# Identity products in TensorE's waits during the opening stage of an audio tower

## The chip, the cores and the metric

The kernel runs on one NeuronCore of a Trainium2 chip. The metric is device time in microseconds (us) of one execution, and lower is better. Five engines work side by side: TensorE (PE in the profile; its weight loads are listed apart as PEld), VectorE (DVE), ScalarE (ACT), GpSimd (POOL) and SyncE (SP), which issues most of the transfers. They meet at semaphores alone.

## The reference

Three blocks run one after the other on `x` of shape (8, 64, 1000):

```python
xp = x.reshape(B, C, S, 200)                       # 5 patches of 200 samples per channel
fr = jnp.fft.rfft(xp, axis=-1)
feats = jnp.concatenate([jnp.abs(fr), jnp.angle(fr)], axis=-1)
h = gelu(feats @ W1 + b1) @ W2 + b2                # tokens, 320 per batch row
...
dt = jnp.mean(jnp.clip(jnp.exp(log_dt), 0.0001, 1.0))
inv_term = jnp.linalg.inv(I - 0.5 * dt * A)        # 32 x 32
A_bar = (I + 0.5 * dt * A) @ inv_term
state = jnp.tanh(state @ A_bar.T + ub_t)           # 320 steps
...
h_new = z * h + (1.0 - z) * c                      # gated recurrence, 320 steps
```

The second and third block each add their result to `h`. The change touches the first block and the start of the inverse.

## The kernel before, in words

Every engine has a program written out by hand, and each runs its own list strictly in that order; what comes first anywhere is set by that order and by the semaphores.

The patches come in four pieces of `x` (`g` = 0 to 3). For a piece, VectorE (GpSimd for pieces 2 and 3) folds each patch into an even and an odd half (`even_odd`, L472 to L474), TensorE turns these into columns (`transposes`, L1217; two halves `h` of the piece, 6 and 4 products), ScalarE and VectorE copy them from PSUM (`evenT` L658, `oddT` L902), and TensorE multiplies them with a cosine and a sine table (`spectra`, L1231). Magnitude and angle are then worked out on three engines: VectorE reads the spectra (`imag` L908, `neghalf` L910), ScalarE takes absolute values, squares and roots, VectorE forms a reciprocal (`rdenom` L926), GpSimd multiplies (`absim` L568), ScalarE takes the arctangent, GpSimd and VectorE put the angle together (`angT` L937). ScalarE loads a new function table for each of root, arctangent and gelu (L688 with `ACT_TABLE_LOAD`).

The inverse is found by a Newton iteration with 40 steps of two halves each: `newton(i)` is one small product on TensorE (L1245 for even `i`, L1247 for odd `i`), and ScalarE copies its result back (L694, L697, L698) before the next half can start. The first eight halves (`EARLY`) stand in the opening stage, the others are spread between the products of the first network.

These are `up` (L1372: features times `W1`, magnitude half and angle half, 128 hidden units by up to 384 tokens) and `down` (L1387: times `W2`), in groups `n` = 0 to 6 of tokens and seven pieces `m` of hidden units. With the first `up` the opening stage ends. From about 180 us on, the gated recurrence with its 320 steps fills the rest of the span.

TensorE's list begins with `WARM` = 26 transposes of the identity matrix into PSUM bank 6, which nobody reads (L1251); they need the identity alone, which GpSimd has made by 1.6 us. Behind them stand the transposes of piece 0, which need the first load. The products are float32; a product that is no transpose stands in the profile as two matmuls.

Of the kernel before, what the change touches and what calls it, by code (L numbers as in the profile page):

```python
# [33 lines left out]
TINY_POWER = 1e-34  # L34
EPS = 1e-5
NEWTON = 40
WARM = 26
EARLY = 8

XT_PIECE, SKIP_PIECE = 4, 6  # L40
# [29 lines left out]
def audio_tower(nc, x, W1, b1, W2, b2, A, Bm, C, D, log_dt, W_out, b_out,  # L70
# [31 lines left out]
    with ExitStack() as ctx:  # L102
        def sb(name, shape, dt=F32):
            return ctx.enter_context(nc.sbuf_tensor(name, shape, dt))

        def sem(name):
            return ctx.enter_context(nc.semaphore(name))
# [7 lines left out]
        ident = sb("ident", [128, 128])  # L115
# [105 lines left out]
        def bank(i, p=128, w=512):  # L221
            return ps[0:p, i, 0:w]
# [3 lines left out]
        def ps_patT(k, g, h):  # L226
            return bank(k + (4 if (g, h) == (0, 1) else 0), KP - 1 if k else KP + 1)

        def ps_re(g, h):
            return bank(6 if (g, h) == (0, 1) else 2, NF, HT)  # L230

        def ps_im(g, h):
            return bank(7 if (g, h) == (0, 1) else 3, NF, HT)
# [42 lines left out]
        im_read = sem("im_read")  # L276
# [84 lines left out]
        def patches(h):  # L361
            s0, s1 = (0, S0) if h == 0 else (S0, NS)
            return s0, s1, slice(128 * s0, 128 * s1)
# [78 lines left out]
        def newton_bank(i):  # L442
            at = [key[0] for key, j in SLOTS.items() if j == i]
            b = 3 if i < EARLY else 2 if at[0] % 2 else 7
            return bank(b, 128, N), bank(b, 128, 2 * N)
# [760 lines left out]
        def _(pe):  # L1206
            mm, tr = nc.tensor.matmul, nc.tensor.transpose
            def transposes(g, h):
                s0, s1, cols = patches(h)
                if h == 0:  # L1210
                    pe.wait_ge(parts_done[g], 1)
                if 2 * g + h > 1:
                    pe.wait_ge(patT0_copied, 2 * g + h)
                    pe.wait_ge(patT1_copied, 2 * g + h)
                for k, part in enumerate((even, odd)):
                    for sg in range(s0, s1):
                        last = tr(ps_patT(k, g, h)[:, (sg - s0) * 128:(sg - s0 + 1) * 128],  # L1217
                                  part[:, g, sg, :], ident[:])
                last.then_inc(patT_psum, 1)

            def spectra(g, h):
                if h == 0:
                    if g == 0:
                        pe.wait_ge(dft_in, 48)
                    pe.wait_ge(patT0_copied, 2 * g + 2)
                    pe.wait_ge(patT1_copied, 2 * g + 2)
                if 2 * g + h > 1:
                    pe.wait_ge(re_read, 2 * g + h)
                    pe.wait_ge(im_read, 2 * g + h)
                for dst, table, part in ((ps_re(g, h), cos_sb, evenT), (ps_im(g, h), sin_sb, oddT)):  # L1230
                    last = mm(dst, table[:], part[:, h * HT:(h + 1) * HT], start=True, stop=True)  # L1231
                last.then_inc(spec_psum, 1)

            def wait_newton(i):
                if i % 2:
                    pe.wait_ge(xy_done, i + 1)
                else:
                    pe.wait_ge(dn_done, i // 2 + 1)

            def newton(i):  # L1240
                ps_nt, ps_nx = newton_bank(i)
                if i:
                    wait_newton(i - 1)
                if i % 2 == 0:
                    mm(ps_nt, step_w[:], Xn[:], start=True, stop=True).then_inc(nt_psum, 1)  # L1245
                else:
                    mm(ps_nx, DY[:], DY[:, 0:2 * N], start=True, stop=True).then_inc(nx_psum, 1)  # L1247

            pe.wait_ge(consts, 1)
            for _ in range(WARM):  # L1250
                tr(bank(6)[:, 0:128], ident[:], ident[:])  # L1251
            transposes(0, 0)
            transposes(0, 1)
            pe.wait_ge(su_dve, 2)
            pe.wait_ge(consts, 16)
            mm(bank(3)[:, 0:1], ones_row[:], dtsum[:], start=True, stop=True).then_inc(su_pe, 1)
# [2 lines left out]
            pe.wait_ge(su_dve, 9)  # L1259
            mm(bank(5)[0:N, 0:1], ones_sq[:], sqsum[:], start=True, stop=True).then_inc(sq_psum, 1)  # L1260
            spectra(0, 1)
            pe.wait_ge(su_dve, 11)
            pe.wait_ge(bf_ident, 4)
            pe.wait_ge(im_read, 1)
# [2 lines left out]
            pe.wait_ge(re_read, 1)  # L1267
            mm(bank(2)[:, 0:3 * DM], ones_row[:], vec_rows[:].rearrange("p a d -> p (a d)"),
               start=True, stop=True).then_inc(su_pe, 1)
            newton(1)  # L1270
            tr(bank(5)[:, 0:128], Wout_sb[:], ident[:]).then_inc(su_pe, 1)
            newton(2)
            transposes(1, 0)
            for i in range(3, 6):
                newton(i)
            pe.wait_ge(rows_in, 16 * 8)
            tr(bank(4)[:, 0:32], bias_rows[:], ident[0:32, 0:32]).then_inc(bias_psum, 1)
            for i in range(6, EARLY):
                newton(i)
            pe.wait_ge(su_act, 6)  # L1280

            def ssm_input(c):
# [352 lines left out]
```

## Time and profile before

| what | value |
|---|---|
| median of 3 runs | 895.92 us (894.9 to 898.41) |
| the profiled execution's own time | 894.79 us |
| its span, first to last instruction | 893.0 us |
| TensorE busy | 829.9 us, 93% of the span |
| mean granted TensorE clock | 0.581 of full speed |

The span leaves out 1.79 us around the instructions. The granted clock is 1 at 2.4 GHz and 0.5 at 1.2 GHz, the two levels that occur; a value between them is a mean over a stretch in which the level changed.

### The profile page before, as it was taken

The page shows a single profiled execution, that of the slowest core. Times are in us where ns is not written, and L with a number is a line of the kernel's source. Part 1 is how long each engine was busy: PE and PEld are TensorE (multiplying, and loading weights), DVE is VectorE, ACT ScalarE, POOL GpSimd, SP SyncE. Part 2 cuts the span into 40 slices and gives each one's busy share as a digit, 9 for nine tenths or more (in the row PEclk, how much of TensorE's full clock was granted, in tenths as well). Part 3 has the DMA queues.
Part 4 walks back from the last instruction along what each step waited for, and adds up shares of the span by engine and source line. Part 5 has one row for each costly group of instructions (what it writes and reads, how often), then busy time and mean ns, then how long its engine had stood idle before and what let it go on. Part 6 is the DMA issues. An engine that isn't in the chain of part 4 may idle for free.

```text
span 893.0 us, 40450 instructions
## 1 busy us (share of the span) xinstructions
PE 829.9 (93%) x17013; PEld 700.3 (78%) x17013; DVE 578.6 (65%) x3480; ACT 369.8 (41%) x2016; POOL 89.7 (10%) x205
## 2 busy tenths in 40 slices
PE   7889999989999999999999999999999998988875
PEld 5667666778888888888888888888888887877765
DVE  5243527376676776767767777677667777676654
ACT  5465766433343433433434334334333343343222
POOL 4212204110000000100000001000000000000000
PEclk6699999955555555555555555555555555555555
DMA  7100000000000000000000000000000000000000
GB/s 173 35 1 1 1 1 1 1 3 3 7 3 7 6 4 6 7 3 7 4 6 7 3 7 6 4 6 3 7 6 4 6 7 3 6 4 5 6 3 8
DMA packets 7452, 8.51 MB, mean 10 GB/s; under 512 B 1343, under 2 KB 6557, under 8 KB 7271
## 3 DMA queue, kind: packets, MB, share of 16 engines
q1 hardware_dynamic: 6965, 5.92, 2.8%
q8 instruction: 133, 2.18, 1.0%
q14 instruction: 48, 0.39, 0.1%
q0 software_dynamic: 256, 0.01, 0.0%
q10 hardware_dynamic: 50, 0.00, 0.0%
HBM read 4.62 MB, written 1.31 MB: 7 GB/s over the span
## 4 chain that ended last, share of the span: by engine, by line
PE 85%; ACT 6%; DVE 4%; issue 3%; DMA 1%; POOL 0%; POOLq 0%
PE ps L1511 42%; PE ps L1517 11%; PE ps L1313 8%; PE ps L1372 5%; PE ps L1423 3%; PE ps L1387 3%; PE ps L1525 3%; DVE h_hi L478 2%; PE ps L1431 2%; ACT addend L866 2%; PE ps L1295 1%; PE ps L1302 1%; PE ps L1283 1%; PE ps L1231 1%; PE ps L1247 1%
## 5 line engine op out<-in xcount | busy, mean ns | idle before, releaser
L1511 PE MATMUL ps<-h_hi,w_first 128*128 128x8 f16 x2552 | 267.3, 170 | 28.4 <-DVE h_hi L478 28.0
L1511 PEld LDWEIGHTS ps<-h_hi,w_first 128*128 128x128 f16 x2552 | 219.9, 104 | 90.9 <-DVE h_hi L478 90.9
L1511 PE MATMUL ps<-h_hi,w_rest 128*128 128x8 f16 x5104 | 276.3, 168 | 0.0
L1511 PEld LDWEIGHTS ps<-h_hi,w_rest 128*128 128x128 bf16 x5104 | 240.6, 105 | 0.1
L856 ACT ACTIVATE tanh_r<-ps 128x16 f32<-128x16 f32 x320 | 58.6, 183 | 252.3 <-PE ps L1517 251.7
L1517 PE MATMUL ps<-h_lo,w_first 128*128 128x8 f16 x2560 | 160.0, 168 | 0.1
L1511 PE MATMUL ps<-rh_hi,w_first 128*128 128x8 f16 x1276 | 136.6, 173 | 12.1 <-DVE rh_hi L1133 1.0
L1511 PEld LDWEIGHTS ps<-rh_hi,w_first 128*128 128x128 f16 x1276 | 109.6, 104 | 39.0 <-DVE rh_hi L1133 1.3
L1511 PE MATMUL ps<-rh_hi,w_rest 128*128 128x8 f16 x2552 | 138.6, 168 | 0.0
L478 DVE TENSOR_TENSOR_SCAN h_hi<-coef,addend 128x32 f16<-128x32 f32 x320 | 73.1, 228 | 85.7 <-ACT addend L866 85.7
L1511 PEld LDWEIGHTS ps<-rh_hi,w_rest 128*128 128x128 bf16 x2552 | 121.8, 105 | 0.0
L1517 PEld LDWEIGHTS ps<-h_lo,w_first 128*128 128x128 f16 x2560 | 117.9, 105 | 0.4 <-DVE h_lo L1156 0.2
L1133 DVE SCALAR_TENSOR_TENSOR rh_hi<-tanh_r,hseq 128x16 f16<-128x16 f32 x320 | 56.1, 175 | 90.0 <-ACT tanh_r L856 85.2
L866 ACT ACTIVATE addend<-ps 128x16 f32<-128x16 f32 x320 | 59.5, 186 | 110.1 <-PE ps L1517 100.7
L858 ACT ACTIVATE tanh_z<-ps 128x16 f32<-128x16 f32 x320 | 58.6, 183 | 77.7 <-PE ps L1517 77.7
L1313 PE MATMUL ps<-x2T,WuT 128*128 128x128 f32 x240 | 90.0, 480 | 0.3 <-ACT ps L780 0.3
L1517 PE MATMUL ps<-rh_lo,w_first 128*128 128x8 f16 x1280 | 79.3, 168 | 0.7 <-DVE rh_lo L1138 0.7
L602 POOL COPY hchunk<-hseq 128x128 f32<-128x128 f32 x40 | 11.7, 293 | 522.1 <-DVE h_lo L1156 522.1
L478 DVE TENSOR_TENSOR_SCAN hseq<-coef,addend 128x32 f32<-128x32 f32 x320 | 63.8, 199 | 0.0
L1156 DVE TENSOR_TENSOR h_lo<-hseq,h_hi 128x16 f16<-128x16 f32 x320 | 56.0, 175 | 11.0
L1138 DVE TENSOR_TENSOR rh_lo<-rh,rh_hi 128x16 f16<-128x16 f32 x320 | 55.9, 175 | 10.9
L739 ACT ACTIVATE states<-ps 128x8 f32<-128x8 f32 x320 | 55.2, 173 | 17.2 <-PE ps L1295 16.6
(211 smaller groups left out, 1421.6 us busy)
## 6 DMA issues: line engine op xcount, KB each, us to landing
x_sb<-in_x SPq DMA_DIRECT2D x4, 500.0 KB
out<-res SPq DMA_DIRECT2D x20, 64.0 KB, 2.0
W_sb<-in_L_tok_W SPq DMA_DIRECT2D x1, 606.0 KB
W_sb<-in_L_tok_W SPq DMA_DIRECT2D x1, 384.0 KB
wnat<-in_L_ffn_Wwr SPq DMA_DIRECT2D x1, 256.0 KB, 5.4
wnat<-in_L_ffn_Wwz SPq DMA_DIRECT2D x1, 256.0 KB, 11.2
wnat<-in_L_ffn_Ww SPq DMA_DIRECT2D x1, 256.0 KB, 10.5
wunat<-in_L_ffn_Wur SPq DMA_DIRECT2D x1, 128.0 KB, 6.9
```

The costliest lines, as they stand in the source:

```text
L478: return v.tensor_tensor_scan(out=dst, data0=coef[:].rearrange("p s i -> p (s i)"), data1=addend[:].rearrange("p s i -> p (s i)"), initial ...
L739: a.activation(states[:, c % 2, k * NB:(k + 1) * NB], ps_s[:, c % 2, k, :], ACT.Tanh, scale=1.0 / S_SCALE).then_inc(s_done, 1)
L856: a.activation(halves(tanh_r[:]), gate(c, j, 0), ACT.Tanh, scale=0.5 / G_SCALE).then_inc(r_done, 1)
L858: a.activation(halves(tanh_z[:]), gate(c, j, 1), ACT.Tanh, scale=0.5 / G_SCALE).then_inc(z_done, 1)
L866: a.activation(halves(addend[:, :, 0]), gate(c, j, 2), ACT.Tanh, scale=1.0 / G_SCALE).then_inc(c_done, 1)
L1133: v.scalar_tensor_tensor(out=rh_hi[:], in0=tanh_r[:], scalar=1.0, in1=h_prev, op0=ALU.add, op1=ALU.mult).then_inc(rh_hi_done, 1)
L1138: v.tensor_tensor(rh_lo[:], rh[:], rh_hi[:], ALU.subtract).then_inc(rh_lo_done, 1)
L1156: v.tensor_tensor(h_lo[:], hseq[:, j, :, 1], h_hi[:, :, 1], ALU.subtract).then_inc(h_lo_done, 1)
L1313: mm(gate_columns(g, c)[:, m].rearrange("p t b -> p (t b)"), WuT[:, i, :], x2T[:], start=False, stop=True, skip_group_check=True)
L1372: last = mm(ps_hid[p % 2][0:k, 0:nq * CT], W1_sb[:, half, m * 128:m * 128 + k], feats[:, t0:t0 + nq * CT], start=half == 0, stop=half == 1)
L1511: mm(gate(c, j, g, m), w[:, m * 128:(m + 1) * 128], state[:, k * NB:(k + 1) * NB], start=False, stop=False, skip_group_check=True)
L1517: last = mm(gate(c, j, g, m), w_first[:, g, k, m * 128:(m + 1) * 128], state[:, k * NB:(k + 1) * NB], start=False, stop=k == KH - 1, skip_ ...
```

## The change

`WARM` grows from 26 to 52, and groups of 6 or 12 more identity transposes (`BUSY` = 6) are put at ten places of TensorE's opening list: 78 products, 104 more with those of `WARM`. They write PSUM banks that are free at that place and signal nothing. Ahead of the first group into bank 7, TensorE now waits until VectorE has read that bank (`im_read`, 2). No other engine's list changes.

```diff
-WARM = 26
+WARM = 52
+BUSY = 6
...
+            def busy(count, b):
+                for _ in range(count):
+                    tr(bank(b)[:, 0:128], ident[:], ident[:])
+
             pe.wait_ge(consts, 1)
-            for _ in range(WARM):
-                tr(bank(6)[:, 0:128], ident[:], ident[:])
+            busy(WARM, 6)
             transposes(0, 0)
             transposes(0, 1)
+            busy(BUSY, 6)
             pe.wait_ge(su_dve, 2)
...
             spectra(0, 1)
+            busy(2 * BUSY, 0)
             pe.wait_ge(su_dve, 11)
...
                start=True, stop=True).then_inc(su_pe, 1)
+            busy(BUSY, 0)
             newton(1)
             tr(bank(5)[:, 0:128], Wout_sb[:], ident[:]).then_inc(su_pe, 1)
+            busy(BUSY, 0)
             newton(2)
             transposes(1, 0)
             for i in range(3, 6):
+                busy(BUSY, 4)
                 newton(i)
...
             for i in range(6, EARLY):
+                if i == 6:
+                    pe.wait_ge(im_read, 2)
+                busy(2 * BUSY, 7)
                 newton(i)
+            busy(BUSY, 7)
             pe.wait_ge(su_act, 6)
```

TensorE's list at its beginning, before (L1251 the identity products, L1217 the transposes of piece 0, L1256 the sum for `dt`, L1231 the spectra, L1260 a norm, L1245 the first Newton half):

```order
L1251 MATMUL ps<-ident 128x128 x26
L1217 MATMUL ps<-ident,even 101x128 x3
L1217 MATMUL ps<-ident,odd 99x128 x3
L1217 MATMUL ps<-ident,even 101x128 x2
L1217 MATMUL ps<-ident,odd 99x128 x2
L1256 MATMUL ps<-dtsum,ones_row 128x1
```

The same place in the change, where line numbers are one to thirteen higher (L1252 is the identity product, L1218 the transposes):

```order
L1252 MATMUL ps<-ident 128x128 x52
L1218 MATMUL ps<-ident,even 101x128 x3
L1218 MATMUL ps<-ident,odd 99x128 x3
L1218 MATMUL ps<-ident,even 101x128 x2
L1218 MATMUL ps<-ident,odd 99x128 x2
L1252 MATMUL ps<-ident 128x128 x6
L1261 MATMUL ps<-dtsum,ones_row 128x1
```

There are now 52 products ahead of the first transposes and 6 between them and the sum for `dt`.

TensorE's list at the end of the opening stage, before, from Newton half 5 on (L1277 turns the bias rows; the last row is the first `up` product):

```order
L1247 MATMUL ps<-DY 128x64
L1277 MATMUL ps<-ident,bias_rows 128x32
L1245 MATMUL ps<-Xn,step_w 128x32
L1247 MATMUL ps<-DY 128x64
L1372 MATMUL ps<-magT,W_sb 128x384
```

The same place in the change:

```order
L1248 MATMUL ps<-DY 128x64
L1286 MATMUL ps<-ident,bias_rows 128x32
L1252 MATMUL ps<-ident 128x128 x12
L1246 MATMUL ps<-Xn,step_w 128x32
L1252 MATMUL ps<-ident 128x128 x12
L1248 MATMUL ps<-DY 128x64
L1252 MATMUL ps<-ident 128x128 x6
L1385 MATMUL ps<-magT,W_sb 128x384
```

Twelve identity products stand ahead of Newton half 6, twelve between halves 6 and 7, and six ahead of the first `up` product.

## Rows read from the trace of the kernel before

**Rows 1.** The page: TensorE's busy time, and its granted clock in 40 slices (tenths).

```profile
PE 829.9 (93%) x17013; PEld 700.3 (78%) x17013; DVE 578.6 (65%) x3480; ACT 369.8 (41%) x2016; POOL 89.7 (10%) x205
...
PEclk6699999955555555555555555555555555555555
```

**Rows 2.** Busy time by stretch: us, PE, PEld, DVE, ACT, POOL (count), clock, DMA.

```profile
8.00:10.00 2.00, 1.30 (x6) 1.31 (x7) 1.04 (x4) 0.00 (x0) 1.69 (x4) 0.56 0.93 204
10.00:28.00 18.00, 13.96 (x42) 9.11 (x40) 15.71 (x31) 12.51 (x35) 4.51 (x6) 0.50 0.78 185
28.00:38.00 10.00, 9.49 (x27) 6.84 (x28) 1.19 (x4) 2.95 (x12) 1.99 (x2) 0.50 0.01 2
38.00:40.00 2.00, 2.00 (x12) 1.60 (x11) 0.00 (x0) 0.58 (x3) 0.00 (x0) 0.76 0.00 0
```

**Rows 3.** The chain that ended last, opening stage: start us, us, what.

```profile
10.34 1.52 ACT evenT L658 x2
...
25.15 1.28 ACT L688
...
28.71 1.39 PE ps L1372 x2
```

**Rows 4.** Timeline of TensorE, opening stage: start us, us, instruction, [idle before].

```profile
1.65 4.59 PE L1251 MATMUL ps<-ident 128*128 128x128 f32 x26 [1.65 <-POOL ident L528]
8.70 0.96 PE L1217 MATMUL ps<-ident,even 128*101 128x128 f32 x3 [2.46 <-DVE odd L474]
...
27.11 0.64 PE L1245 MATMUL ps<-Xn,step_w 128*128 128x32 f32 x2 [2.04 <-ACT DY L698]
...
28.50 1.59 PE L1372 MATMUL ps<-magT,W_sb 101*128 101x384 f32 x2
```

**Rows 5.** Timeline of VectorE and ScalarE around the spectra of piece 0.

```profile
14.58 0.49 DVE L908 TENSOR_SCALAR imag<-ps 101x320 f32<-101x320 f32 x1 [0.22 <-PE ps L1231]
...
16.54 0.47 ACT L680 ACTIVATE magT<-power 101x320 f32<-101x320 f32 x1 [0.30 <-DVE power L915]
...
17.16 0.49 DVE L908 TENSOR_SCALAR imag<-ps 101x320 f32<-101x320 f32 x1 [0.65 <-PE ps L1231]
...
17.62 0.49 DVE L910 TENSOR_SCALAR neghalf<-ps 101x320 f32<-101x320 f32 x1
```

**Rows 6.** The chain that ended last, from the first `up` product on.

```profile
31.80 0.85 PE ps L1217 x4
...
37.25 0.27 PE ps L1245 x2
37.52 1.44 PE ps L1387 x6
...
39.19 0.70 PE ps L1372 x2
...
42.06 0.72 PE ps L1387 x6
42.79 0.17 PE ps L1245 x2
```

**Rows 7.** Timeline of TensorE at later places.

```profile
61.27 0.71 PE L1387 MATMUL ps<-W_sb,hid 128*128 128x128 f32 x4 [2.49 <-DVE h L1008]
...
112.53 0.38 PE L1217 MATMUL ps<-ident,odd 128*99 128x128 f32 x2
112.75 0.50 PE L1387 MATMUL ps<-W_sb,hid 128*128 128x128 f32 x3
...
148.92 0.66 PE L1336 MATMUL ps<-ident,wunat 128*128 128x128 f32 x4 [1.70 <-ACT wT L750]
```

**Rows 8.** Busy time by stretch, later places (columns as in rows 2).

```profile
62.00:64.00 2.00, 2.00 (x11) 1.66 (x11) 1.97 (x6) 0.87 (x4) 0.65 (x1) 0.71 0.06 12
...
68.00:70.00 2.00, 2.00 (x10) 1.86 (x10) 1.61 (x3) 1.34 (x2) 0.80 (x1) 0.58 0.00 0
...
148.00:150.00 2.00, 1.08 (x9) 1.08 (x10) 0.94 (x1) 1.98 (x5) 1.90 (x3) 1.00 0.00 0
```

## The prediction

> **What bounds the kernel now.** I read the page first. TensorE is busy for 93% of the span, but its granted clock is at half speed in most slices [rows 1], and a busy share says nothing on how fast the engine works. The late slices are the gated recurrence, which the change does not reach. What it can reach is the low clock in the second slice, so I asked for the stretches there. The mean of 0.56 from 8 to 10 us puts the fall from 2.4 to 1.2 GHz at 8.24 us (0.24 us at full, 1.76 us at half), the stretch to 38 us is at 0.50 throughout, and the mean of 0.76 from 38 to 40 us puts the rise at 38.96 us [rows 2].
>
> The chain of waits then says where that half clock costs time. Up to 28.7 us the chain runs through many engines, copies of ScalarE and a table load among them [rows 3]; TensorE has 13.96 us of work in the 18 us from 10 to 28 us, and much of it hides behind the others. From the first up product on it is TensorE nearly alone: 9.49 us of 10 busy at half clock [rows 2], while VectorE has 1.19 us and ScalarE 2.95 us. There each us of product time is a us of the kernel.
>
> The timeline of TensorE shows why the clock is low. The 26 identity products start at 1.65 us and end at 6.24 us, the first transposes stand 2.46 us later at 8.70 us [rows 4], and in between nothing runs. The clock fell in that gap and 0.46 us before the transposes, and waits such as the 2.04 us ahead of 27.11 us follow.
>
> **The 26 products more at the start.** One transpose takes 0.213 us at half clock (0.85 for 4 [rows 6]) and 0.11 us at full (two in 112.53 to 112.75 [rows 7]). The 26 took 4.59 us in all; 15 at 0.213 and 11 at 0.11 make 4.4 us and the tail of the last one, so the clock rose after some 15 of them, at 4.85 us, whatever the mean over a stretch shows before the first recorded change. With 52, 37 run at 0.11: they end at 4.85 + 4.07 = 8.92 us, 0.22 us after the load lets the transposes go. I take that as the cost. If the rise comes only after all of the first 26, they end at 1.65 + 5.54 + 2.86 = 10.05 us, 1.35 us late; that is the bound on the bad side.
>
> **The waits up to Newton half 6.** If the clock stays full, the six transposes of the first half take 0.66 us in place of 1.28 us, so the copy `evenT` at 10.34 us [rows 3] can start 0.62 − 0.22 = 0.40 us earlier. Behind it VectorE waited twice on spectra, 0.22 and 0.65 us [rows 5]. Both spectra halve and both waits go; but of the second only 0.17 us comes through, because ScalarE's root ends at 17.01 us, its next absolute value takes some 0.44 us (an estimate from its neighbour's 0.47 us), and `neghalf` at 17.62 us needs that. Sum: 0.40 + 0.22 + 0.17 = 0.79 us. From there the reciprocals, GpSimd, the arctangents and a table load at 25.15 us [rows 3] run without TensorE, and the groups of 6 (0.66 us each) and of 12 (1.3 us) on TensorE lie in waits that these leave. If the second load has not landed earlier, the 0.40 us is lost; if the copies start sooner because a product also drains faster, 0.15 us comes on top. Bounds: 0.39 to 0.94 us. Newton half 6 starts at 26.3 us in place of 27.11 us.
>
> **The end of the stage.** Twelve products now stand between halves 6 and 7, where ScalarE's copy would be ready earlier, and six more ahead of the first up product; TensorE does them in order, needed or not. From half 6 to the up product it took 28.50 − 27.11 = 1.39 us [rows 4]. Now: 0.17 for half 6 [rows 6], 1.32, 0.17 for half 7, 0.66, together 2.32 us. That loses 0.93 us and eats the 0.79 us: the first up product starts 0.1 us later than before, at 28.6 us.
>
> **The up and down products.** From 28.71 us to the next shown up product at 39.19 us is 10.48 us at half clock. On the chain stand four up products of 1.39 to 1.44 us, which take 0.70 us at full [rows 3, 6]: 2.8 us saved. Three down products of one piece take 0.72 in place of 1.44 us: 0.72. Four transposes: 0.85 − 0.44 = 0.41. Six Newton pieces, the typical one 0.27 and at full 0.17 [rows 6]: 0.6. Together 4.5 us. ScalarE's copies in this stretch (2.95 us in 10 [rows 2]) fit: the same pattern at full clock behind 39 us stays on TensorE's rows. Half of 10.48 bounds it at 5.2 us, and if Newton's copies show through once more, 4.0 us.
>
> **Sum.** 4.5 − 0.1 = 4.4 us off the profiled execution's own 894.79 us (span 893.0 and 1.79 around it): 890.4 us. The runs' median is 1.13 us above that execution, so 891.5 us. As the executions with more time have, if it is the clock, more half-speed work to lose, I take 0.2 us off: 891.3 us. The products themselves cost nothing as long as they end before what the next product waits for; where they don't is the 0.93 us above.
>
> **Does the clock hold?** The rows have it fall after gaps of 2.46 us [rows 4] and 2.49 us, and stay at full across one of 1.70 us [rows 7, 8]. Of the waits in the opening stage the one ahead of half 6 was the longest with 2.04 us [rows 4]; the twelve products take 1.32 us of it, and with the products ahead of them ending up to 0.7 us sooner at full clock it comes to 0.7 to 1.4 us, below 1.70. Against it speaks that the work between the waits is thin: Newton halves of 0.17 us and a product with one row of weights, where the gap that held had full products on both sides.
>
> **Rivals.** *The clock lapses between the waits.* Then the late groups run at half pace. Half 6 starts at 26.3 us, 0.27 for it, 2.56 for the twelve, 0.27 and 1.28 for the six: the first up product at 30.7 us, 2.2 us later than before. Eighteen products in a row are more than the 15 after which the clock rose at the start, so it is back by then: 4.5 − 2.2 = 2.3 us gained, 893.6 us. If it were not, 2.2 us are lost, 898.1 us.
>
> *A later low stretch goes, or moves.* After the 2.49 us gap the clock is low from 62.84 us (mean 0.71) to 69.68 us (mean 0.58) [rows 8] and TensorE is busy throughout; at full that work takes 3.4 us less. The change doesn't touch that gap, but the fall comes 1.6 us after its end, so a shift of 4 us may place it otherwise: 891.3 − 3.4 = 887.9 us. The same can happen the other way, at the 1.70 us gap that held: 894.7 us.
>
> *Identity transposes don't raise or hold the clock.* Then 52 take 11.09 us, the transposes start at 12.74 us, 4.0 us late, the six ahead of the sum for `dt` add 1.28 us, and the end of the stage 2.56 + 1.28 − 0.6 = 3.2 us: 8.5 us slower, 904 us. It decides for slower once more than 4.5 us stand. The pace of the first 26 speaks against it. The Trainium skill has this rule (TensorE: Matmul & The Clock Gate, "Part 4: PE-mode transpose"): the full clock does not engage for transpose-mode work, which does not count as busy in the same way. By that rule the 904 us would hold; the trace disagrees, since transposes alone went from 0.213 to 0.11 us apiece.
>
> *Nothing comes through*, because another engine takes the place of TensorE from 28.6 us on: 895.9 us. ScalarE's 2.95 us in 10 speak against it.
>
> **How the numbers follow.** About 0.5%, 4.5 us, is what a measurement of this kernel tells from no change. The clock holds and 4 to 5.5 us come through: 0.58, and as 891.4 us is the edge, 0.32 of it faster and 0.26 within. Low stretch gone on top: 0.14, faster. Lapse, or a new low stretch: 0.22, within. Identity products without effect on the clock: 0.04, slower. Nothing comes through: 0.02, within. So faster 0.46, within 0.5% 0.50, slower 0.04. The likeliest case has 891.3 us, on its own 890 to 892.5 us. The range for 8 in 10 is 887.9 to 894.5 us: it takes in the late rise (1.1 us) and most of the lapse, and leaves out the 904 us and the ends of the phase cases.
>
> **What would show it.** In the changed profile the stretches from 10 to 38 us should stand at a clock near 1, the first transposes near 8.9 us, the first up product near 28.6 us and the one at 39.19 us [rows 6] near 34.8 us. A clock of 0.5 anywhere between 15 and 30 us means the lapse. Transposes at 0.213 us behind the first 15 mean the rule of the page. The forecast is wrong if the first up product comes behind 29.5 us, or if the stretch behind it takes over 7 us at full clock.

## The result, and the profile after

The change has a median of 892.48 us (892.02 to 894.55, 20 runs), the kernel before in the same rounds 895.96 us (892.12 to 898.63, 20 runs). The ratio is 0.9969, with an interval of 0.9956 to 0.9981: 0.31% or 3.5 us faster. That is clear of the noise, less than the 0.5% that the prediction takes for no change, and inside the range that was forecast. The profiled execution of the change took 892.20 us (span 890.4 us), 2.59 us less than that of before.

The page of the change: busy time of the engines, and TensorE's granted clock in 40 slices.

```profile
PE 831.1 (93%) x17117; PEld 704.6 (79%) x17117; DVE 578.3 (65%) x3480; ACT 371.2 (42%) x2016; POOL 89.4 (10%) x205
...
PEclk9979999955555555555555555555555555555555
```

The second slice, which stood at 6 before [rows 1], now has 9; the third, which had 9, has 7. The same stretches as in [rows 2] and some later ones say where that is. The columns are those of [rows 2].

```profile
8.00:10.00 2.00, 2.00 (x20) 2.00 (x19) 1.02 (x4) 0.00 (x0) 1.69 (x4) 1.00 0.88 226
10.00:28.00 18.00, 15.88 (x115) 12.79 (x114) 15.76 (x31) 12.57 (x35) 5.01 (x6) 1.00 0.79 179
28.00:38.00 10.00, 9.51 (x57) 7.07 (x56) 1.15 (x4) 3.88 (x16) 1.52 (x2) 1.00 0.01 2
...
57.00:58.00 1.00, 0.97 (x6) 0.97 (x7) 1.00 (x1) 0.00 (x0) 0.43 (x1) 0.69 0.03 8
...
58.00:66.00 8.00, 8.00 (x31) 7.24 (x31) 4.35 (x13) 5.26 (x12) 4.92 (x8) 0.50 0.01 2
...
67.00:68.00 1.00, 1.00 (x6) 0.71 (x6) 0.00 (x0) 0.20 (x1) 0.00 (x0) 0.69 0.00 0
...
146.00:150.00 4.00, 3.67 (x15) 3.33 (x16) 3.49 (x4) 2.71 (x6) 3.85 (x5) 0.57 0.00 0
```

From 8 to 38 us the clock stands at 1.00, where it stood at 0.50 to 0.56. TensorE gets 57 matmuls done from 28 to 38 us, 10 of them identity products, in place of 27, and is as busy as before: the busy share says nothing here, the count does. But two later stretches are worse. The clock falls at 57.38 us (0.69 of the slice from 57 to 58 is 0.38 us at full) and is back at 67.62 us: 10.24 us at 1.2 GHz, where before had 6.84 (62.84 to 69.68). And from 146 to 150 us it stands at 0.57, which is 3.44 us at half clock, where before held it [rows 8].

The timeline of TensorE in the change, to be read beside [rows 4, 7]:

```profile
1.65 8.09 PE L1252 MATMUL ps<-ident 128*128 128x128 f32 x52 [1.65 <-POOL ident L529]
9.57 0.49 PE L1218 MATMUL ps<-ident,even 128*101 128x128 f32 x3
...
26.61 0.41 PE L1246 MATMUL ps<-Xn,step_w 128*128 128x32 f32 x2 [1.25 <-ACT DY L699]
26.86 1.51 PE L1252 MATMUL ps<-ident 128*128 128x128 f32 x12
28.20 0.33 PE L1248 MATMUL ps<-DY 128*128 128x64 f32 x2
28.37 0.82 PE L1252 MATMUL ps<-ident 128*128 128x128 f32 x6
29.04 0.81 PE L1385 MATMUL ps<-magT,W_sb 101*128 101x384 f32 x2
34.77 0.86 PE L1385 MATMUL ps<-magT,W_sb 101*128 101x384 f32 x2
...
57.03 0.92 PE L1400 MATMUL ps<-W_sb,hid 128*128 128x128 f32 x4 [2.50 <-DVE h L1009]
...
146.33 1.12 PE L1349 MATMUL ps<-ident,wunat 128*128 128x128 f32 x4 [1.70 <-ACT wT L751]
```

What starts where, in the profiled executions of before and of the change (us; the third row is the up product behind the stretch of 10.48 us, whose part on the chain starts at 39.19 [rows 6]):

| place | before | change | change ahead by |
|---|---|---|---|
| first transposes | 8.70 | 9.57 | −0.87 |
| first up product | 28.50 | 29.04 | −0.54 |
| third up product on the magnitude | 39.03 | 34.77 | 4.26 |
| down product behind the long gap [rows 7] | 61.27 | 57.03 | 4.24 |
| first product of `xlnT` and `BbarT` (input of the second block) | 138.9 | 136.3 | 2.6 |
| first product of the recurrence (`rh_hi`) | 181.1 | 179.8 | 1.3 |
| end of the span | 893.0 | 890.4 | 2.6 |

So 4.26 us are won by the third up product, 1.6 of them go back behind the gap of 2.50 us, another 1.3 around the gap of 1.70 us, and 1.3 come back in the recurrence, which the change doesn't touch. The last number has to be kept apart from the effect of the change.

### The profile page after: what moved, and what is told of

Read it like the earlier page. It is cut to its first block, busy times and chain, and to the rows that moved or that the text cites. A ratio compares the mean times of both kernels' runs of the same rounds, so it can differ in the third digit from the quotient of the medians.

```text
span 890.4 us, 40658 instructions
## 1 busy us (share of the span) xinstructions
PE 831.1 (93%) x17117; PEld 704.6 (79%) x17117; DVE 578.3 (65%) x3480; ACT 371.2 (42%) x2016; POOL 89.4 (10%) x205
## 4 chain that ended last, share of the span: by engine, by line
PE 86%; ACT 6%; DVE 5%; issue 3%; POOL 0%; POOLq 0%
PE ps L1524 42%; PE ps L1530 11%; PE ps L1326 8%; PE ps L1385 5%; PE ps L1436 3%; PE ps L1400 3%; PE ps L1538 3%; DVE h_hi L479 2%; PE ps L1444 2%; ACT addend L867 2%; PE ps L1308 1%; PE ps L1315 1%; PE ps L1296 1%; PE ps L1252 1%; PE ps L1248 1%
## 5 line engine op out<-in xcount | busy, mean ns | idle before, releaser
L603 POOL COPY hchunk<-hseq 128x128 f32<-128x128 f32 x40 | 11.7, 293 | 521.0 <-DVE h_lo L1157 521.0
L1139 DVE TENSOR_TENSOR rh_lo<-rh,rh_hi 128x16 f16<-128x16 f32 x320 | 56.1, 175 | 10.9
```

The lines of the kernel that those rows point to most:

```text
L1139: v.tensor_tensor(rh_lo[:], rh[:], rh_hi[:], ALU.subtract).then_inc(rh_lo_done, 1)
```

## The experiments

Theory A is the prediction's: the products keep the clock up through the opening, and the up and down products there gain 4 to 5 us. Rivals: (B) the longer start alone does it, or the groups alone; (C) the products that stand at the end of the stage cost what they bring; (D) what is won is lost again in later low stretches. Ratios are to the kernel before on the same chip. Edits are shown against the change, if nothing else is said.

**The kernel before, again** (no edit).

> The kernel before, unchanged, profiled and timed once more. Theory (the low clock from 8 to 39 us costs about 4 us in the up products, and low stretches behind it come and go): ratio 1.000, the clock falls again in the gap of 2.5 us before the first transposes or soon behind it and rises again between 32 and 42 us; the low stretches behind it need not lie where they lay. Rival (the place of the low stretches is fixed by the program): rise at 38.96 us and falls at 62.9 us again, within 0.1 us.

Median 893.26 us (891.12 to 896.85), ratio 0.9988 [0.9966, 1.001]. Its profiled execution took 896.85 us, and its clock did something else than that of the first profile:

```profile
10.00:12.00 2.00, 1.04 (x7) 0.84 (x6) 1.92 (x6) 1.37 (x3) 0.00 (x0) 0.68 1.07 166
12.00:44.00 32.00, 27.88 (x78) 18.53 (x77) 14.77 (x29) 14.72 (x47) 6.51 (x7) 0.50 0.41 97
44.00:46.00 2.00, 2.00 (x13) 1.81 (x12) 0.49 (x1) 1.03 (x4) 0.00 (x0) 0.79 0.00 0
```

It fell at 10.72 us and came back at 44.84 us (0.79 of 44 to 46 is 1.16 us at full), 5.9 us later than in [rows 2] and later than expected; its span is 2.0 us longer. The gap ahead of the first transposes was shorter than in [rows 4], since the clock rose later and the 26 products took longer, and the fall came behind it all the same:

```profile
9.02 0.57 PE L1217 MATMUL ps<-ident,even 128*101 128x128 f32 x3 [1.57 <-DVE odd L474]
```

One kernel has executions with low stretches of different length, so what the change saves differs from one execution of before to the next: at the down product behind the long gap this one stands at 63.84 us and the first at 61.27, so that the 57.03 us of the change are 6.8 or 4.2 us ahead. That the runs of before spread over 6.5 us and those of the change, but for one, over 1.1 us, agrees with it.

**The longer start alone, without the groups.**

```diff
-WARM = 26
+WARM = 52
```

(against the kernel before, which has none of the groups)

> Only the 26 more products at the start, none in the waits behind. Theory: the clock is full for the first transposes and both spectra (0.4 to 0.8 us earlier there) and falls in the thin stretch between 15 and 28 us, so the up products run at half pace again: 0 to 1 us faster than before, ratio 0.999 to 1.000. Rival (the start alone does it, the products in the waits are not needed): the clock stays full to the first up product, which starts 0.9 us earlier than in the changed kernel because nothing stands in front of it: 4 to 5 us faster than before, ratio 0.995.

895.42 us, ratio 1.0019 [0.9996, 1.0041]: nothing gained. Its busy time by stretch:

```profile
18.00:20.00 2.00, 1.46 (x7) 1.24 (x8) 2.00 (x2) 1.81 (x5) 0.00 (x0) 0.62 0.54 151
20.00:38.00 18.00, 14.00 (x46) 10.63 (x45) 7.49 (x12) 8.61 (x31) 6.51 (x7) 0.50 0.27 81
38.00:40.00 2.00, 2.00 (x9) 1.44 (x9) 0.00 (x0) 0.56 (x3) 0.00 (x0) 0.76 0.00 0
```

The clock came past the first transposes, fell at 18.5 us and was back at 39 us, as in before. The first up product stood at 27.68 us, 0.8 us earlier than in before, and the third one on the magnitude at 38.24 us, also 0.8 us earlier: against this execution of before, the full clock up to 18.5 us is worth 0.8 us, which the prediction had as 0.79 us, and the up products gained nothing.

**The groups alone, with the 26 products at the start.**

```diff
-WARM = 52
+WARM = 26
```

> The products in the waits, but only 26 at the start, so that the 2.5 us gap ahead of the first transposes is back. Theory: the clock falls near 8 us as before; the groups of 6 and 12 bring it back at some time before 30 us, late groups at half pace cost up to 2.2 us: 2 to 4 us faster than before, ratio 0.996 to 0.998. Rival (once down, the clock comes back only with the up products): first up product near 30.7 us and ratio 1.002.

891.42 us, ratio 0.9969 [0.9949, 0.9989], the same as the change. In the profiled execution, with 889.1 us the fastest of the twelve, the clock did not fall near 8 us, where it was expected to. It rose at 6.61 us, so that the products ended later than in [rows 4] and left a gap of 1.62 us in place of 2.46:

```profile
8.72 0.57 PE L1218 MATMUL ps<-ident,even 128*101 128x128 f32 x3 [1.62 <-DVE odd L475]
```

Over that gap the clock held, up to 57.80 us. B in its first form is out by the kernel before this one: the longer start alone gains nothing, the groups carry the gain. In its second form it stands: by the medians the longer start adds nothing, and in this profile the clock gets over the gap without it.

**The change without the last twelve and six products.**

```diff
             for i in range(6, EARLY):
                 if i == 6:
                     pe.wait_ge(im_read, 2)
-                busy(2 * BUSY, 7)
+                    busy(2 * BUSY, 7)
                 newton(i)
-            busy(BUSY, 7)
```

> The changed kernel without its last 18 products (the 12 between Newton halves 6 and 7 and the 6 ahead of the first up product). Theory: the work left keeps the clock full, and the first up product starts 0.9 to 1.5 us earlier than the 29.04 us of the changed kernel; ratio 0.995 to 0.996 to the kernel before, against 0.997 of the change. Rival (these 18 hold the clock): it falls between 26 and 30 us, the first up products run at half pace, ratio 0.998 to 1.002.

889.13 us, ratio 0.9954 [0.9933, 0.9976]. Ten runs lie from 887.6 to 890.5 us, two at 893.6 and 894.4. In the profiled execution, one of the ten, the first up product runs 2.09 us earlier than in the change, and the clock stands at 1.00 from 8 to 28 us and holds to 56.1 us:

```profile
26.95 0.86 PE L1385 MATMUL ps<-magT,W_sb 101*128 101x384 f32 x2
```

Of the 2.09 us, 0.62 were there before the eighteen are reached (Newton half 6 at 25.99 in place of 26.61 us, after a start that ended 0.62 us earlier, with the transposes at 8.95). The other 1.47 us are what the eighteen cost. In these two executions C is right in size: the eighteen stand in the way. The medians don't tell the two kernels apart (the intervals of the ratio are 0.9933 to 0.9976 and, for the change, 0.9956 to 0.9981).

**The change, again,** on another chip, beside the next three kernels.

> The changed kernel, unchanged, profiled and timed once more on the chip of the other runs. Theory (4 to 5 us won in the up products, and the low stretches after the later gaps of 2.5 and 1.7 us take 1.5 to 3 us back in some executions): the clock is full from its first rise to about 57 us, the third magnitude product stands at 34.3 to 34.8 us, the ratio is 0.996 to 0.997. Rival (the low stretches behind are as long as before, and the up products gain only 2.6 us): the third magnitude product at 36.4 us.

891.23 us against 893.86 for before there, ratio 0.9978 [0.996, 0.9995]. The profile repeats: first up product 28.87 us, clock low from 57.06 to 67.30 us and from 145.81 to 149.22 us, recurrence from 179.6 us on. The twelve runs lie in two groups here, seven from 890.4 to 891.4 us and five from 892.8 to 893.4 us; the profiled one (892.79 us) is of the five. Thirty runs of before on this chip took 890.24 to 900.09 us, against 890.39 to 893.36 for the change: what the change takes away are the long executions of before, and on the fastest it gains next to nothing (on the first chip 892.12 and 892.02 us).

**The change, and the two later gaps filled.** If D is right, products there give back what the later stretches took.

```diff
+GAP = 18
...
+                if i == 3:
+                    busy(2 * BUSY, 3)
...
+                if n == 1 and m == 0:
+                    busy(GAP, 0)
```

(the first in `transpose_weights`, at the 1.70 us gap; the second in `down()`, ahead of the wait on `out_read`, at the 2.50 us gap)

> The changed kernel with 18 identity products in the later gap of 2.5 us (ahead of the first down product of group 1, near 54 us) and 12 in the gap of 1.7 us (near 144.6 us). Theory: both low stretches go, the clock stays full to about 180 us: 4 to 6 us faster than the change, 885.5 to 888 us, ratio 0.990 to 0.992 to the kernel before. Rival (other engines bound the stretch from 57 to 70 us, and the low clock costs little there): within 1 us of the change.

888.44 us (887.81 to 888.82), ratio 0.9931 [0.9902, 0.996], just above what was expected. The groups and the down product behind them, in the timeline:

```profile
54.77 2.13 PE L1253 MATMUL ps<-ident 128*128 128x128 f32 x18
...
57.43 0.71 PE L1405 MATMUL ps<-W_sb,hid 128*128 128x128 f32 x4 [0.53 <-DVE h L1010]
```

The same stretches as in the change, and the tile of the first product behind them:

```profile
58.00:66.00 8.00, 6.93 (x49) 5.78 (x47) 6.21 (x14) 6.24 (x15) 5.15 (x8) 1.00 0.01 3
144.00:150.00 6.00, 5.96 (x39) 4.53 (x38) 5.86 (x8) 4.34 (x14) 4.64 (x5) 1.00 0.01 3
```

```profile
L1297 PE MATMUL ps<-xlnT,BbarT x2: 275/326/377, 133.1 to 133.3; 128*128 128x128 f32 x2
```

The gap is down from 2.50 to 0.53 us, the clock is full from 7.0 to 174.3 us without a break, and the product of `xlnT` and `BbarT` stands at 133.1 us. In the change on the same chip it stood at 136.1 us: 3.0 us, although this execution was 0.6 us behind at the first up product. At the recurrence it is 4.2 us (175.4 for 179.6), and so it stays to the end of the span. D is shown: on this pair of executions the later low stretches cost the change 4.2 us. By the medians it is 2.8 us (891.23 and 888.44), since the change's profiled execution is one of its longer ones. A part of that before paid as well, since its clock was low there for 6.84 us.

**Both: the gaps filled, without the last eighteen.**

```diff
-                busy(2 * BUSY, 7)
+                if i == 6:
+                    busy(2 * BUSY, 7)
                 newton(i)
-            busy(BUSY, 7)
```

(against the kernel with the gaps filled)

> As the one before (18 and 12 products in the two later gaps), without the 18 products at the end of the opening stage. Theory: the two gains add, 1 to 1.5 us faster than with the tail, ratio 0.988 to 0.991. Rival (the tail is needed in some executions to hold the clock): the median is no better than with the tail, and the spread is wider.

887.43 us, ratio 0.9952 [0.9923, 0.9981]. Eight runs lie from 886.2 to 887.5 us, four from 893.9 to 895.8. The profiled one is of the eight, with the clock full from 7.6 to 174.9 us; the four had a mean clock of 0.591 to 0.592 in place of 0.597 to 0.599. Without the eighteen the clock is lost in some executions; none of the six runs with them took so long. That in the four it was lost at the end of the opening is argued from the next kernel, they were not profiled.

**The same with 44 products at the start.**

```diff
-WARM = 52
+WARM = 44
```

(against the kernel just above)

> As the one before, with 44 products at the start in place of 52. Theory: where the clock rises late, the 52 end behind the load (first transposes at 9.57 us in the changed kernel's trace); 44 end at 8.0 to 8.7 us, so the first transposes stand at 8.7 us always: 0 to 0.5 us faster in the median. Rival (the gap that 44 leave lets the clock fall): first spectra at half pace, 0.5 to 1 us slower.

890.91 us (886.85 to 898.02), ratio 0.9965 [0.994, 0.9991]. The first transposes stand at 9.04 us, and not at 8.7 us as expected. The profile caught the lapse, and a second fall far behind it:

```profile
26.00:28.00 2.00, 1.64 (x6) 1.10 (x7) 1.34 (x3) 0.67 (x5) 1.61 (x3) 0.84 0.27 84
28.00:30.00 2.00, 2.00 (x6) 1.24 (x5) 0.00 (x0) 0.19 (x1) 0.97 (x1) 0.50 0.03 6
...
106.00:112.00 6.00, 6.00 (x22) 4.22 (x23) 0.00 (x0) 1.55 (x6) 0.00 (x0) 0.50 0.01 3
```

The clock fell at 27.36 us (0.84 of 26 to 28), just as the up products begin at 27.04 us. The third one on the magnitude stands at 34.49 us; in the last kernel below, which begins its up products at 27.07 us at full clock, it stands at 32.91: 1.6 us for the lapse. The second low stretch begins at 105.9 us. The timeline has no long wait ahead of either fall, the longest are these:

```profile
26.08 0.41 PE L1247 MATMUL ps<-Xn,step_w 128*128 128x32 f32 x2 [1.26 <-ACT DY L700]
...
103.50 0.71 PE L1405 MATMUL ps<-W_sb,hid 128*128 128x128 f32 x4 [1.13 <-ACT hid L801]
```

They lie 1.3 and 2.4 us ahead of the falls. The same two waits were passed at full clock in the profile of the kernel just above, with 52 products at the start, so they don't explain the falls by themselves.

**The gaps filled, and the end of the opening fitted:** twenty products where TensorE waits for half 6, six in place of twelve between the halves, none ahead of the first up product.

```diff
-                busy(2 * BUSY, 7)
+                busy(20 if i == 6 else BUSY, 7)
                 newton(i)
-            busy(BUSY, 7)
```

(against the change with the gaps filled)

> The kernel with the two later gaps filled, and the end of the opening stage fitted to its waits: 20 products ahead of Newton half 6 (the changed kernel's trace leaves 1.25 us idle behind its 12), 6 in place of 12 between halves 6 and 7, none ahead of the first up product. Theory (what counts is that the waits are filled and nothing is queued past them): the 1.3 us of the tail come back and the clock holds in every execution: 886.5 to 887.5 us, a spread under 2 us, ratio 0.991 to 0.993. Rival (the tail's own work is what holds the clock): some executions at 893 to 896 us again, as without the tail.

886.66 us (886.0 to 888.01, 6 runs) against 895.12 for before there, ratio 0.9919 [0.9893, 0.9944], 0.8% faster. Its timeline:

```profile
23.84 2.40 PE L1253 MATMUL ps<-ident 128*128 128x128 f32 x20
26.62 0.41 PE L1247 MATMUL ps<-Xn,step_w 128*128 128x32 f32 x2 [0.38 <-ACT DY L700]
26.86 0.85 PE L1253 MATMUL ps<-ident 128*128 128x128 f32 x6
27.55 0.33 PE L1249 MATMUL ps<-DY 128*128 128x64 f32 x2
27.72 0.86 PE L1387 MATMUL ps<-magT,W_sb 101*128 101x384 f32 x2
```

Half 6 starts where it does in the change, with 0.38 us of waiting left in place of 1.25, and from half 6 to the first up product it is 1.10 us, less than the 1.39 us of before; with no products there it was 0.96 us (25.99 to 26.95). All six runs lie within 2.0 us, none of them near 893 us. This version is faster than both kernels: its interval ends below that of the change (0.9956 to 0.9981). From the kernel that only fills the gaps (0.9902 to 0.996) the intervals don't tell it apart.

**The fitted kernel with 44 products at the start** (`WARM` = 44).

> As the one before, with 44 products at the start in place of 52. Theory: the first transposes stand at 8.7 to 9.1 us and not at 9.4 to 10.3 us, which is worth 0.3 to 0.9 us where the clock rises late; the clock holds, 886 to 887 us. Rival (fewer products at the start leave the clock low in some executions): a spread of several us, as with 44 and no tail.

886.34 us (885.73 to 887.50, five runs), ratio 0.9915 [0.989, 0.9941]; a sixth run took 973.04 us at a mean clock of 0.513 and is left out. First transposes 8.85 in place of 9.36 us, first up product 27.07 in place of 27.72 us, but the medians are 0.3 us apart and the intervals of the ratio nearly the same. Whether 44 is enough with this end of the stage is open: five runs are few for that.

## Why the prediction came out, step by step

The forecast was 891.3 us, the measurement 892.48. On the profiled execution it was 890.4 against 892.20, that is 1.8 us too fast, and the steps say where.

**The products at the start.** Forecast: the clock rises after 15, the 52 end at 8.92 us, with 10.05 as the bad end. The 52 took 8.09 us to 9.74. With 0.213 and 0.11 us apiece and 0.2 us for the tail that is some 21 at half clock, so it rose at about 6.1 us, and the first transposes came at 9.57, 0.87 us late in place of 0.22. Mis-sized by 0.65 us, inside the bounds. The rise is not a fixed place: the transposes stand at 9.41 us in the second profile of the change, at 8.95 without the eighteen, which are far behind it.

**The waits up to half 6.** Forecast 0.79 us gained, half 6 at 26.3 us. It started at 26.61, so 0.50 us gained with the start 0.65 us later; with a start as forecast (transposes at 8.95) half 6 stood at 25.99, a little better than forecast. The step that the sum named as the next in the way is there: `neghalf` runs at 17.12 us in place of 17.62 [rows 5], and waits for ScalarE's absolute value, no longer for TensorE:

```profile
17.12 0.49 DVE L911 TENSOR_SCALAR neghalf<-ps 101x320 f32<-101x320 f32 x1 [0.46 <-ACT absre L666]
```

**The end of the stage.** From half 6 to the up product 2.32 us were forecast and 2.43 took place (26.61 to 29.04). ScalarE had the copy for half 7 at 27.06 + 0.19 = 27.25 us, and half 7 ran at 28.20, because the twelve were ahead of it:

```profile
27.06 0.19 ACT L695 ACTIVATE DY<-ps 32x32 f32<-32x32 f32 x1 [0.42 <-PE ps L1246]
```

That the eighteen eat the gain of the waits was right, and the kernel without them shows the 1.47 us.

**The up and down products.** The same rows of the chain as in [rows 3, 6], at full clock:

```profile
29.20 0.65 PE ps L1385 x2
30.72 0.44 PE ps L1218 x4
34.02 0.75 PE ps L1400 x6
34.94 0.70 PE ps L1385 x2
```

The stretch is 34.94 − 29.20 = 5.74 us in place of 10.48: 4.74 saved, 4.5 forecast. The up product, the four transposes and the down piece have 0.65, 0.44 and 0.75 us for the 0.70, 0.44 and 0.72 of the sum. At 34.77 us the change is 4.26 us ahead, where 4.4 were forecast. So far the prediction is right in mechanism, and its misses of size cancel out: the start costs 0.65 us more than its term, the waits and the stretch bring more than theirs, and 0.14 us are left.

**"Does the clock hold?" and the rival of the later low stretch.** This is the step that failed. The prediction's likeliest case left the later stretches as they were, and gave a full clock over the 1.70 us gap, on the word of one row [rows 7, 8]. In both profiles of the change the low stretch behind the 2.50 us gap lasted 10.24 us in place of 6.84; the 3.4 us more of half-speed work are 1.7 us, and 1.6 are missing at `BbarT`. And in both the clock was lost in the 1.70 us gap: another 1.3 us. The rival "the other way", which named that gap and 894.7 us, was right in its place and not in its price, 3.4 us; it shared a chance of 0.22 with the lapse.

What such a gap costs differs from profile to profile. The stretches at the fall and the rise behind the 2.50 us gap, with the longer start alone (two rows) and without the last eighteen (two rows):

```profile
58.00:60.00 2.00, 0.32 (x2) 0.00 (x0) 2.00 (x2) 1.94 (x4) 0.00 (x0) 0.86 0.02 4
68.00:70.00 2.00, 2.00 (x12) 2.00 (x11) 0.67 (x1) 1.92 (x5) 1.49 (x2) 0.58 0.00 0
...
56.00:58.00 2.00, 2.00 (x8) 1.67 (x7) 1.87 (x7) 0.60 (x4) 0.86 (x1) 0.52 0.00 0
62.00:64.00 2.00, 2.00 (x12) 1.84 (x11) 1.43 (x3) 1.52 (x2) 0.72 (x1) 0.77 0.00 0
```

The first is low from 59.44 to 69.68 us, 10.24 us, at nearly the place where before had its 6.84 us; the second from 56.08 to 62.92 us, 6.84 us, though its products stand earlier than those of the change. In the seven profiles with this gap open, the stretch lasted 10.24 us in the three whose fall lay inside the gap or at most 0.4 us behind its end, and 6.84 us in the four whose fall came 1.05 to 1.6 us behind it. The 1.70 us gap, open in the same seven, lost the clock in the two profiles of the change and held it in the other five. The prediction's own words, that a shift may place the fall otherwise, fit this; where the fall comes to lie was not controlled in any run.

The 1.3 us that the recurrence took less hid nearly half of the two losses: 0.14 + 1.6 + 1.3 − 1.3 is, but for rounding, the 1.8 us by which the execution missed its forecast. That was luck. Over the twelve profiles of this study the recurrence took 710.6 to 711.9 us, and the two compared here are the two ends.

Other rows show that the length of a gap alone does not decide. Ahead of the first transposes 1.62 us held in the kernel with the groups alone, and 1.57 us were followed by a fall in the second profile of before, which has no groups behind the gap. What else decides was not settled.

**What was compared.** The median gained 3.5 us where the two profiled executions differ by 2.6, because before's profiled execution lay 1.17 us below its median and that of the change 0.28 us. The prediction took 0.2 us for that difference; it was 0.9 us. The 0.7 us more cover a part of the 1.8, and the forecast of the median is 1.2 us too low. It came nearer to the measurement than the forecast of the execution did, and this too was luck.

**The identity products count.** The rival of 904 us, and the rule of the Trainium skill that stood beside it (TensorE: Matmul & The Clock Gate, "Part 4: PE-mode transpose"), are out. By that rule the 52 would have taken 11.1 us at 0.213 us apiece, an estimate; they took 8.09, and the stretches from 8 to 38 us, with all the groups in them, stand at 1.00.

The rival that nothing comes through is out with the 4.74 us of the up and down products, and the lapse with the same stretches at 1.00: in the change's two profiles it did not occur. One profile shows it, that of the kernel with 44 products and without the last eighteen; for the longer runs of the other kernels without the eighteen it is argued, not shown.

## What to carry to other kernels

Work that nobody reads is worth its place only where TensorE waits anyway: put about as many products there as the wait holds (20, 6 and 0 here, in place of 12, 12 and 6), and few or none where the operand would be ready. Follow the clock to the end of the kernel before counting a gain: what was won in the first 40 us here went in part into a longer low stretch 20 us later, and filling the two later gaps and fitting the end of the opening made the gain 0.8% in place of 0.3%. And where executions of one kernel spread by more than the change is worth, profile the kernel before twice; one profile gives one of several prices.

## What the runs showed of the hardware

- At half clock TensorE can be busy nearly throughout and not get its clock back: 9.49 us of 10 from 28 to 38 us [rows 2], and in the second profile of before up to 44.84 us, with full-size products in a row. At the start it came up between 4.8 and 7.6 us in the profiles of this study, behind nothing but identity products back to back.
- The clock also fell without a long gap: in the kernel with the longer start alone at 18.5 us. From 11.7 us on the engine had run the spectra, the norm, Newton halves and a product with one row of weights there, and no wait was over 1.3 us.
- The recurrence took 711.9 and 711.2 us in the two profiles of before, 710.6 and 711.3 in those of the change and 710.9 to 711.6 in the eight others, with the same instructions and the clock at half from about its start on in all of them. Where the 1.3 us come from stays open.
